# Attention on one core: the first head's two score banks in one maximum instruction, and outputs grouped by query halves

## The chip, the core and the metric

The kernel runs on one core of a Trainium2 chip. A core has TensorE (PE, matrix products from SBUF into PSUM), VectorE (DVE), ScalarE (ACT), GpSimd (POOL) and SyncE (SP, which here only issues DMAs). PSUM has eight banks of 512 f32 per partition. The metric is the device time of one execution in microseconds.

## What is computed

The program is a chain of blocks on 4096 tokens of 256 features: an attention block beside a feed-forward block, then a convolution and recurrence with a gated MLP beside a mixture of experts. The change touches the first attention alone:

```
keys    = einsum('bthk,hik->bthi', xd, tokeys) * scale      # 16 heads of 16 features, 4096 tokens
queries = einsum('bthk,hik->bthi', xd, toqueries) * scale
values  = einsum('bthk,hik->bthi', xd, tovalues)
dot  = einsum('bqhs,bkhs->bhqk', queries, keys)             # 4096 x 4096 for each head
attn = softmax(dot, axis=-1)
out  = einsum('bhqk,bkhs->bqhs', attn, values).reshape(b, t, e)
return out @ W_unify + b_unify
```

## The kernel before

**The tiling.** Phases follow each other: front, select, ffn, attention, unify, router, mlp, experts. Attention works on pairs of heads (`NP` = 8) and chunks of `CH` = 512 queries (`NQ` = 8). One pair and one chunk is a *round*, 64 in all; `r` counts rounds inside a group of two pairs, `g` over all. A round has `U` = 16 *units* `u`; a unit takes 256 keys (two key tiles `j` of 128) for the tile products. Loops are written out, so the order on each engine is the order of the code.

**Two streams of scores.** Softmax subtracts the row's maximum, which must be known before the exponentials. So scores are computed twice. `max_part` (L1122) multiplies 128 queries by 512 keys into one of four banks `SA[0..3]` (`scores_q`): banks 0 and 1 are head 0, banks 2 and 3 head 1. DVE reduces each bank to one maximum a query (`reduce_unit`, L1237), and only then may PE refill it (`sa_free`). This stream runs `LEAD` = 24 units ahead, so that it has no work in the last 24 units. At the end of a round's maxima `negative_max` (L1244) reduces 64 partial maxima to 8, POOL splits them in two parts (`split_max`), and SP carries them through HBM into two extra rows of the query operand.

`score_tile` (L1128) then computes the transposed scores, 128 keys by 512 queries, with the maximum subtracted, into one of three banks `ST[0..2]`; ACT turns each into `probs` (`exps`, L1203), four tiles a unit. A max part on one half of PE's rows and a score tile on the other half are issued as a pair and run side by side.

**The output.** `pv_part` (L1137) multiplies probabilities by values into the one bank `OP`. A product has only 32 output rows (16 features, a row of ones for the denominator, padding), and four of them stand side by side in the 128 rows: head times key tile. An even unit has two such blocks of 256 queries (LOW, HIGH), an odd unit one block of all 512 (ALL). The four groups of 32 rows thus hold, for each head, two partial sums over the even and the odd key tiles. At a round's end ACT copies the bank to `O4` (`copy_parts`, L1199); SP moves the odd part to the even part's partitions (`fetch_other_half`), POOL adds the two (`sum_halves`), and SP stores the sum and the denominators (`store`).

**The order on PE** in a unit is: pair, pair (then LOW, if the unit is even), pair (then ALL, if odd), pair (then HIGH, if even). I call the pairs 0 to 3 by the bank of their max part. The copy stands on ACT in unit 0 of the next round, after its third exponential. PE waits for it in unit 1, before ALL.

**After attention**, unify needs the last round's sums: SP stores them, loads the denominators, DVE takes reciprocals, SP spreads them, and SP's queue then goes on to later chunks' loads.

## Time and profile before

| | us |
|---|---|
| median of three runs | 3851.46 (3850.99 to 3851.89) |
| profiled execution, its own time | 3858.98 |
| its span | 3857.2 |
| PE busy | 3690.4 (96%) |
| DVE busy | 3288.7 (85%) |
| ACT busy | 2631.5 (68%) |
| POOL busy | 449.7 (12%) |
| mean granted clock of PE | 0.98 of full speed |

Busy time is the union of an engine's instructions. They overlap on an engine, since the next starts before the last has drained: a mean length is longer than an engine's busy time divided by the count. In the page's grouped rows stand line, engine, operation, output and input, shapes, count, then busy us and mean ns of one, then the engine's idle us just before these instructions and who ended it. A PE product of f32 operands shows as two records, so four products of `pv_part` are eight.

### The profile page before, as it was taken

How to read it: one execution, taken by the hardware profiler on the slowest of the kernel's cores; microseconds unless marked ns; L12 is line 12 of the kernel's file. 1: busy time of each engine (PE TensorE's matmuls, PEld its weight loads, DVE VectorE, ACT ScalarE, POOL GpSimd, SP SyncE). 2: the span in 40 equal slices, each digit the busy share in tenths (PEclk: the TensorE clock that was granted, in tenths of full speed). 3: DMA queues.
4: the chain of work that ended last, by engine and by line, in shares of the span. 5: the costliest groups of instructions: out<-in, count | busy, mean ns of one | idle time of the engine just before them, and what ended most of it. 6: DMA issues, size and time to landing. Idle time of an engine off the chain costs nothing. (4 is left out here: it accounts for less than half of the span.)

```text
span 3857.2 us, 69935 instructions
## 1 busy us (share of the span) xinstructions
PE 3690.4 (96%) x27262; PEld 1976.3 (51%) x27262; DVE 3288.7 (85%) x5513; ACT 2631.5 (68%) x4940; POOL 449.7 (12%) x395
## 2 busy tenths in 40 slices
PE   8799899999999999999999999999998959999998
PEld 6587333333333333333333333333335648888887
DVE  6567799999999999999999999999975747756664
ACT  3455588888888888888888888888886422213332
POOL 0133200000000000000000000000002224102323
PEclk9899899999999999999999999999999979999999
DMA  4910322022122022113112212211012010014332
GB/s 145 239 29 19 111 25 32 6 33 28 11 25 34 10 23 26 20 13 33 24 10 29 28 10 25 35 9 9 8 33 83 0 53 32 30 37 116 79 80 39
DMA packets 301675, 157.47 MB, mean 41 GB/s; under 512 B 218398, under 2 KB 273508, under 8 KB 298801
## 3 DMA queue, kind: packets, MB, share of 16 engines
q1 hardware_dynamic: 289072, 142.49, 19.7%
q0 software_dynamic: 12288, 10.70, 1.7%
q8 instruction: 207, 3.39, 0.4%
q14 instruction: 108, 0.88, 0.1%
HBM read 86.46 MB, written 64.18 MB: 39 GB/s over the span
## 5 line engine op out<-in xcount | busy, mean ns | idle before, releaser
L1203 ACT ACTIVATE probs<-attention_scores_t_sums 128x512 f32<-128x512 f32 x4096 | 2120.1, 599 | 336.0 <-PE attention_scores_t_sums L1128 335.6
L1237 DVE TENSOR_REDUCE max_parts<-attention_scores_q_sums 128x1 f32<-128x512 f32 x2016 | 1212.5, 681 | 24.2 <-PE attention_scores_q_sums L1122 24.1
L1237 DVE TENSOR_REDUCE attention_max_parts<-attention_scores_q_sums 128x1 f32<-128x512 f32 x1984 | 1191.7, 681 | 9.0 <-PE attention_scores_q_sums L1122 9.0
L1128 PE MATMUL attention_scores_t_sums<-q_operand,k_operand 50*128 50x512 f32 x2048 | 732.4, 447 | 21.6 <-ACTq L1217 13.8
L1128 PE MATMUL attention_scores_t_sums<-attention_q_operand,attention_k_operand 50*128 50x512 f32 x2048 | 724.9, 446 | 6.5 <-ACT probs L1203 6.5
L1122 PE MATMUL attention_scores_q_sums<-attention_k_operand,attention_q_operand 48*128 48x512 f32 x2048 | 726.2, 444 | 3.3
L1122 PE MATMUL attention_scores_q_sums<-k_operand,q_operand 48*128 48x512 f32 x1952 | 695.9, 446 | 3.1
L1137 PE MATMUL attention_o_psum_sums<-probs,v_heads 128*32 128x256 f32 (+1 forms) x6144 | 602.7, 464 | 0.0
L1137 PE MATMUL attention_o_psum_sums<-probs,attention_v_heads 128*32 128x256 f32 (+1 forms) x6152 | 601.4, 463 | 0.0
L1122 PEld LDWEIGHTS attention_scores_q_sums<-attention_k_operand,attention_q_operand 48*128 48x128 f32 x2048 | 324.6, 184 | 525.7 <-DVE max_parts L1237 205.2
L1122 PEld LDWEIGHTS attention_scores_q_sums<-k_operand,q_operand 48*128 48x128 f32 x1952 | 311.3, 185 | 504.3 <-DVE max_parts L1237 200.8
L1128 PEld LDWEIGHTS attention_scores_t_sums<-attention_q_operand,attention_k_operand 50*128 50x128 f32 x2048 | 338.8, 184 | 43.2 <-ACT probs L1203 38.7
L1128 PEld LDWEIGHTS attention_scores_t_sums<-q_operand,k_operand 50*128 50x128 f32 x2048 | 341.7, 185 | 36.0 <-ACT probs L1203 20.4
L1294 POOL TENSOR_TENSOR o_parts<-o_parts,o_other_half 128x512 f32<-128x512 f32 x65 | 83.2, 1280 | 1531.5 <-DMA o_other_half<-o_parts 1531.5
L1137 PEld LDWEIGHTS attention_o_psum_sums<-probs,v_heads 128*32 128x32 f32 x6144 | 121.1, 108 | 216.4 <-issue 168.0
L1137 PEld LDWEIGHTS attention_o_psum_sums<-probs,attention_v_heads 128*32 128x32 f32 x6152 | 121.3, 108 | 215.3 <-issue 167.1
L1862 ACT ACTIVATE mlp_silu<-mlp_gate_sums,mlp_b_gate 128x512 f32<-128x512 f32 x64 | 44.1, 689 | 221.8 <-PE mlp_gate_sums L118 221.8
L118 PE MATMUL experts_out_sums<-experts_w_low,experts_hidden_high 128*128 128x256 f32 x512 | 144.8, 283 | 0.0
L118 PE MATMUL experts_out_sums<-experts_w_high,experts_hidden_high 128*128 128x256 f32 x512 | 143.6, 280 | 0.0
L118 PE MATMUL experts_out_sums<-experts_w_high,experts_hidden_low 128*128 128x256 f32 x512 | 143.6, 280 | 0.0
L2124 ACT ACTIVATE experts_hidden<-experts_hidden_sums,experts_b 128x512 f32<-128x512 f32 x64 | 43.5, 686 | 127.4 <-PE experts_hidden_sums L118 103.5
L2124 ACT ACTIVATE experts_hidden<-experts_hidden_sums,first_expert_b 128x512 f32<-128x512 f32 x64 | 43.5, 687 | 121.4 <-PE experts_hidden_sums L118 121.0
(321 smaller groups left out, 4617.6 us busy)
## 6 DMA issues: line engine op xcount, KB each, us to landing
o_other_half<-o_parts SPq DMA_DIRECT2D x130, 64.0 KB, 2.0
expert_rows<-attention_empty_rows SPq DMA_DIRECT2D x16, 516.0 KB, 5.5
v_scratch<-value_chunk SPq DMA_DIRECT2D x16, 512.0 KB, 4.9
w_whole<-in_L_ffn_ew SPq DMA_DIRECT2D x8, 1024.0 KB, 7.1
experts_w_whole<-in_L_ffn_ew SPq DMA_DIRECT2D x8, 1024.0 KB, 5.6
q_operand<-q_scratch SPq DMA_DIRECT2D x24, 256.0 KB, 4.8
k_operand<-k_scratch SPq DMA_DIRECT2D x24, 256.0 KB, 6.6
attention_q_operand<-q_scratch SPq DMA_DIRECT2D x24, 256.0 KB, 4.8
```

The lines of the kernel that those rows point to most:

```text
L118: mm = nc.tensor.matmul(out, lhs[l], rhs[r], start=first and n == 0, stop=last and n == 2)
L1122: nc.tensor.matmul(SA[2 * h + j][:, :], QOP[b][64 * h:64 * h + ROWS, qt * P:(qt + 1) * P], KOP[b][64 * h:64 * h + ROWS, key:key + CH], sta ...
L1128: nc.tensor.matmul(ST[bank_n][:, :], KOP[b][64 * h:64 * h + ROWS + 2, kt * P:(kt + 1) * P], QOP[b][64 * h:64 * h + ROWS + 2, c * CH:(c + 1 ...
L1137: mm = nc.tensor.matmul(OP[32 * (2 * h + t % 2):32 * (2 * h + t % 2) + 32, queries], VH[b][:, kt, h, :], PR[:, u % 4 * 4 + t, queries], st ...
L1203: nc.scalar.activation(PR[:, tile, :], ST[bank_n][:, :], ACT.Exp).then_inc(st_free, 1)
L1237: nc.vector.tensor_reduce(MPART[par][:, h, u // 4, part:part + 1], SA[b][:, :], AX.X, ALU.max)\
L1294: nc.gpsimd.tensor_tensor(self.O4[par][:, :], self.O4[par][:, :], self.OB[:, :], ALU.add).then_inc(self.summed, 1)
L1862: nc.scalar.activation(G[m % 2], GP[m % 2][:, :], ACT.Silu, bias=BG[:, m:m + 1])\
L2124: nc.scalar.activation(HF[m % 2][:, :], HP[m % 2][:, :], ACT.Relu, bias=B1[k][:, m:m + 1])\
```

## The change

The four `scores_q` banks become one tile of four banks. The maxima of banks 0 and 1 are taken by one instruction of 2 x 512 elements (`reduce_first`), which waits for both banks and frees both. Banks 2 and 3 keep an instruction each (`reduce_rest`). `negative_max` of a round moves behind `reduce_first` of the next round's first unit.

The four row groups of `OP` become head times *query half* (side) in place of head times key tile, and `OP` is 256 columns wide. Both key tiles are summed in PE. An even unit's two blocks are now the key tiles 0 and 1; an odd unit has both, eight products of 256 columns in place of four of 512. With no partial sums left, `fetch_other_half`, `sum_halves` and the tile `OB` go; `store` waits for the copy and issues eight DMAs in place of four. The copy takes 256 columns and stands behind the fourth exponential of unit 0.

```diff
--- before.py
+++ after.py
...
         ST = [ps(f"scores_t{b}") for b in range(NB)]
-        SA = [ps(f"scores_q{b}") for b in range(4)]
-        OP = ps("o_psum")
+        SA = ps("scores_q", [P, 4 * CH])
+        OP = ps("o_psum", [P, CH // 2])
...
-        LOW, HIGH, ALL = slice(0, CH // 2), slice(CH // 2, CH), slice(0, CH)
-        BLOCKS = ({(0, 1): LOW, (1, 1): HIGH}, {(1, 0): ALL})
+        BLOCKS = ({(0, 1): (0,), (1, 1): (1,)}, {(1, 0): (0, 1)})
...
-                    outs.fetch_other_half(sp, g, r % 2)
...
-                    outs.sum_halves(nc, pool, g, r % 2)
...
                 pe.wait_ge(sa_free, 4 * s + 2 * h + j + 1)
-                nc.tensor.matmul(SA[2 * h + j][:, :], QOP[b][64 * h:64 * h + ROWS, qt * P:(qt + 1) * P],
+                nc.tensor.matmul(SA[:, (2 * h + j) * CH:(2 * h + j + 1) * CH], QOP[b][64 * h:64 * h + ROWS, qt * P:(qt + 1) * P],
                                  KOP[b][64 * h:64 * h + ROWS, key:key + CH], start=True, stop=True)\
                     .then_inc(sa_ready, 1)
...
-            def pv_part(b, u, exps, queries):
+            def pv_part(b, u, exps, key_tiles):
 
                 pe.wait_ge(st_free, NB + exps)
-                for t in range(4):
-                    h, kt = 1 - t // 2, 2 * u + t % 2
-                    mm = nc.tensor.matmul(OP[32 * (2 * h + t % 2):32 * (2 * h + t % 2) + 32, queries], VH[b][:, kt, h, :],
-                                          PR[:, u % 4 * 4 + t, queries], start=(u == 0 and queries.start == 0),
-                                          stop=(u == U - 1 and queries.stop == CH))
-                if queries.stop == CH:
+                for j in key_tiles:
+                    for n in range(4):
+                        h, side = 1 - n // 2, n % 2
+                        mm = nc.tensor.matmul(OP[64 * h + 32 * side:64 * h + 32 * side + 32, :], VH[b][:, 2 * u + j, h, :],
+                                              PR[:, u % 4 * 4 + 2 * (1 - h) + j, side * (CH // 2):(side + 1) * (CH // 2)],
+                                              start=(u == 0 and j == 0), stop=(u == U - 1 and j == 1))
+                if j == 1:
                     mm.then_inc(pv_done, 1)
...
-                            if u == 0 and t == 2:
+                            if u == 0 and t == 3:
                                 copy_parts(r % 2, i * NQ + r // 2, 4 + g * U)
...
-            def reduce_unit(par, u, s):
-                for b in range(4):
-                    h, part = b // 2, 2 * (u % 4) + b % 2
-                    dve.wait_ge(sa_ready, 4 * s + b + 1)
-                    nc.vector.tensor_reduce(MPART[par][:, h, u // 4, part:part + 1], SA[b][:, :], AX.X, ALU.max)\
-                        .then_inc(sa_free, 1)
+            def reduce_first(par, u, s):
+                first = 2 * (u % 4)
+                dve.wait_ge(sa_ready, 4 * s + 2)
+                nc.vector.tensor_reduce(MPART[par][:, 0, u // 4, first:first + 2], SA[:, 0:2 * CH].rearrange("p (j k) -> p j k", j=2),
+                                        AX.X, ALU.max).then_inc(sa_free, 2)
+
+            def reduce_rest(par, u, s):
+                first = 2 * (u % 4)
+                for j in range(2):
+                    dve.wait_ge(sa_ready, 4 * s + j + 3)
+                    nc.vector.tensor_reduce(MPART[par][:, 1, u // 4, first + j:first + j + 1], SA[:, (2 + j) * CH:(3 + j) * CH],
+                                            AX.X, ALU.max).then_inc(sa_free, 1)
...
-                        if not (last and s_round >= HALF):
-                            reduce_unit(s_round % 2, s_unit, s)
-                            if s_unit == U - 1:
-                                negative_max(s_round % 2, s, g + (u + LEAD) // U)
+                        has_max = not (last and s_round >= HALF)
+                        if has_max:
+                            reduce_first(s_round % 2, s_unit, s)
+                        if s_unit == 0 and not (last and s_round > HALF):
+                            negative_max((s_round - 1) % 2, s - 1, g + (u + LEAD) // U - 1)
+                        if has_max:
+                            reduce_rest(s_round % 2, s_unit, s)
...
-    def fetch_other_half(self, sp, g, par):
+    def store(self, sp, att_scratch, den_scratch, g, par, pair, c):
         sp.wait_ge(self.copied, g + 1)
         for h in range(2):
-            sp.dma_start(self.OB[64 * h:64 * h + 32, :], self.O4[par][64 * h + 32:64 * h + 64, :]).then_inc(self.rows_in, 16)
-
-    def sum_halves(self, nc, pool, g, par):
-        pool.wait_ge(self.rows_in, 32 * (g + 1))
-        pool.wait_ge(self.copied, g + 1)
-        nc.gpsimd.tensor_tensor(self.O4[par][:, :], self.O4[par][:, :], self.OB[:, :], ALU.add).then_inc(self.summed, 1)
-
-    def store(self, sp, att_scratch, den_scratch, g, par, pair, c):
-        sp.wait_ge(self.summed, g + 1)
-        for h in range(2):
-            sp.dma_start(att_scratch[bass.ds(pair * (2 * D) + h * D, D), c * CH:(c + 1) * CH],
-                         self.O4[par][64 * h:64 * h + D, :]).then_inc(self.stored[par], 16)
-            sp.dma_start(den_scratch[bass.ds(pair * 2 + h, 1), c * CH:(c + 1) * CH],
-                         self.O4[par][64 * h + D:64 * h + D + 1, :]).then_inc(self.stored[par], 16)
+            for side in range(2):
+                row, queries = 64 * h + 32 * side, slice(c * CH + side * (CH // 2), c * CH + (side + 1) * (CH // 2))
+                sp.dma_start(att_scratch[bass.ds(pair * (2 * D) + h * D, D), queries],
+                             self.O4[par][row:row + D, :]).then_inc(self.stored[par], 16)
+                sp.dma_start(den_scratch[bass.ds(pair * 2 + h, 1), queries],
+                             self.O4[par][row + D:row + D + 1, :]).then_inc(self.stored[par], 16)
```

On DVE, `x` rows merge equal neighbours. This is the program around the end of one round's maxima, before:

```order
L1237 TENSOR_REDUCE max_parts<-attention_scores_q_sums 128x1 x32
L1244 TENSOR_REDUCE attention_neg_max<-max_parts 128x8
L1237 TENSOR_REDUCE attention_max_parts<-attention_scores_q_sums 128x1 x64
L1244 TENSOR_REDUCE attention_neg_max<-attention_max_parts 128x8
L1237 TENSOR_REDUCE max_parts<-attention_scores_q_sums 128x1 x20
L1250 RECIPROCAL recip_den<-denominators 128x32
```

And after, two units on either side of the end of the second round:

```order
L1235 TENSOR_REDUCE attention_max_parts<-attention_scores_q_sums 128x2
L1242 TENSOR_REDUCE attention_max_parts<-attention_scores_q_sums 128x1 x2
L1235 TENSOR_REDUCE attention_max_parts<-attention_scores_q_sums 128x2
L1242 TENSOR_REDUCE attention_max_parts<-attention_scores_q_sums 128x1 x2
L1235 TENSOR_REDUCE max_parts<-attention_scores_q_sums 128x2
L1249 TENSOR_REDUCE attention_neg_max<-attention_max_parts 128x8
L1242 TENSOR_REDUCE max_parts<-attention_scores_q_sums 128x1 x2
```

A unit is three maxima (L1235, then two of L1242) in place of four (L1237). The step to `neg_max` (now L1249) stands one instruction further on, between the next round's two-bank maximum and its one-bank ones.

On PE, an odd unit from its pair 2 on (`scores_q2`) and an even unit up to its pair 2, before:

```order
L1122 MATMUL attention_scores_q2_sums<-k_operand0,q_operand0 128x512
L1128 MATMUL attention_scores_t1_sums<-q_operand0,k_operand0 128x512
L1137 MATMUL attention_o_psum_sums<-probs,v_heads0 32x512 x4
L1122 MATMUL attention_scores_q3_sums<-k_operand0,q_operand0 128x512
L1128 MATMUL attention_scores_t2_sums<-q_operand0,k_operand0 128x512
L1122 MATMUL attention_scores_q0_sums<-k_operand0,q_operand0 128x512
L1128 MATMUL attention_scores_t0_sums<-q_operand0,k_operand0 128x512
L1122 MATMUL attention_scores_q1_sums<-k_operand0,q_operand0 128x512
L1128 MATMUL attention_scores_t1_sums<-q_operand0,k_operand0 128x512
L1137 MATMUL attention_o_psum_sums<-probs,v_heads0 32x256 x4
```

The same place after:

```order
L1120 MATMUL attention_scores_q_sums<-k_operand0,q_operand0 128x512
L1126 MATMUL attention_scores_t1_sums<-q_operand0,k_operand0 128x512
L1136 MATMUL attention_o_psum_sums<-probs,v_heads0 32x256 x8
L1120 MATMUL attention_scores_q_sums<-k_operand0,q_operand0 128x512
L1126 MATMUL attention_scores_t2_sums<-q_operand0,k_operand0 128x512
L1120 MATMUL attention_scores_q_sums<-k_operand0,q_operand0 128x512
L1126 MATMUL attention_scores_t0_sums<-q_operand0,k_operand0 128x512
L1120 MATMUL attention_scores_q_sums<-k_operand0,q_operand0 128x512
L1126 MATMUL attention_scores_t1_sums<-q_operand0,k_operand0 128x512
L1136 MATMUL attention_o_psum_sums<-probs,v_heads0 32x256 x4
```

The pairs and the places of the blocks stay; the odd unit's block has eight products of 256 columns in place of four of 512.

On ACT, around the copy in a round's unit 0, before:

```order
L1203 ACTIVATE probs<-attention_scores_t1_sums 128x512
L1203 ACTIVATE probs<-attention_scores_t2_sums 128x512
L1203 ACTIVATE probs<-attention_scores_t0_sums 128x512
L1199 COPY o_parts0<-attention_o_psum_sums 128x512
L1203 ACTIVATE probs<-attention_scores_t1_sums 128x512
L1203 ACTIVATE probs<-attention_scores_t2_sums 128x512
```

And after:

```order
L1202 ACTIVATE probs<-attention_scores_t1_sums 128x512
L1202 ACTIVATE probs<-attention_scores_t2_sums 128x512
L1202 ACTIVATE probs<-attention_scores_t0_sums 128x512
L1202 ACTIVATE probs<-attention_scores_t1_sums 128x512
L1198 COPY o_sides0<-attention_o_psum_sums 128x256
L1202 ACTIVATE probs<-attention_scores_t2_sums 128x512
```

The copy is half as wide and has changed places with the exponential behind it.

## Rows read from the trace of the kernel before

**Rows 1.** Windows, 500 us of attention: length, then busy us (x instructions) by engine.

```profile
1500.00:2000.00 500.00, 495.71 (x4102) 195.46 (x4103) 494.95 (x837) 430.67 (x834) 21.91 (x39) 1.00 0.18 21
```

**Rows 2.** The page's part 5 (its columns are told above): maxima, and loads for the output sums.

```profile
L1237 DVE TENSOR_REDUCE max_parts<-attention_scores_q_sums 128x1 f32<-128x512 f32 x2016 | 1212.5, 681 | 24.2 <-PE attention_scores_q_sums L1122 24.1
L1237 DVE TENSOR_REDUCE attention_max_parts<-attention_scores_q_sums 128x1 f32<-128x512 f32 x1984 | 1191.7, 681 | 9.0 <-PE attention_scores_q_sums L1122 9.0
...
L1137 PEld LDWEIGHTS attention_o_psum_sums<-probs,attention_v_heads 128*32 128x32 f32 x6152 | 121.3, 108 | 215.3 <-issue 167.1
```

**Rows 3.** Tile `attention_neg_max`, POOL's reader: durations in ns, first and last start in us.

```profile
L1097 POOL TENSOR_TENSOR attention_neg_max_split<-attention_neg_max,attention_zero x63: 202/203/206, 452.0 to 2870.5; 128x8 fp32r<-128x8 f32 x63
```

**Rows 4.** Timeline of DVE, 1504 to 1695 us: start, length, instruction, [idle before <-releaser].

```profile
1504.61 23.40 DVE L1237 TENSOR_REDUCE max_parts<-attention_scores_q_sums 128x1 f32<-128x512 f32 x39
1528.31 15.04 DVE L1237 TENSOR_REDUCE max_parts<-attention_scores_q_sums 128x1 f32<-128x512 f32 x25 [0.30 <-PE attention_scores_q_sums L1122]
1543.39 0.22 DVE L1244 TENSOR_REDUCE attention_neg_max<-max_parts 128x8 f32<-128x64 f32 x1
1543.52 23.40 DVE L1237 TENSOR_REDUCE attention_max_parts<-attention_scores_q_sums 128x1 f32<-128x512 f32 x39
...
1582.43 12.04 DVE L1237 TENSOR_REDUCE max_parts<-attention_scores_q_sums 128x1 f32<-128x512 f32 x20
1594.38 0.34 DVE L1250 RECIPROCAL recip_den<-denominators 128x32 f32<-128x32 f32 x1
1594.64 11.38 DVE L1237 TENSOR_REDUCE max_parts<-attention_scores_q_sums 128x1 f32<-128x512 f32 x19
```

**Rows 5.** Timeline of DVE in the phase before attention.

```profile
372.26 1.23 DVE L883 TENSOR_REDUCE ffn_lead_max_parts<-ffn_scores_q_sums 128x2 f32<-128x1024 f32 x1 [1.27 <-PE ffn_scores_q_sums L783]
373.40 0.68 DVE L900 TENSOR_TENSOR ffn_gelu_low<-ffn_gelu,ffn_gelu_high 128x512 fp32r<-128x512 f32 x1
```

**Rows 6.** Timeline of all engines, 1524 to 1529 us: units 0, 1 and 2 of a round.

```profile
1524.13 0.39 PE L1122 MATMUL attention_scores_q_sums<-attention_k_operand,attention_q_operand 48*128 48x512 f32 x1
...
1524.46 0.64 PE L1137 MATMUL attention_o_psum_sums<-probs,attention_v_heads 128*32 128x256 f32 x8
...
1525.03 0.49 PE L1122 MATMUL attention_scores_q_sums<-attention_k_operand,attention_q_operand 48*128 48x512 f32 x1
...
1525.22 0.59 ACT L1199 COPY o_parts<-attention_o_psum_sums 128x512 f32<-128x512 f32 x1 [0.26 <-PE attention_o_psum_sums L1137]
...
1526.36 0.49 PE L1128 MATMUL attention_scores_t_sums<-attention_q_operand,attention_k_operand 50*128 50x512 f32 x1 [0.18 <-ACT probs L1203]
...
1526.78 1.06 PE L1137 MATMUL attention_o_psum_sums<-probs,attention_v_heads 128*32 128x512 f32 x8
...
1527.78 0.50 PE L1122 MATMUL attention_scores_q_sums<-attention_k_operand,attention_q_operand 48*128 48x512 f32 x1
...
1528.12 0.40 PE L1122 MATMUL attention_scores_q_sums<-attention_k_operand,attention_q_operand 48*128 48x512 f32 x1
...
1528.31 1.29 DVE L1237 TENSOR_REDUCE max_parts<-attention_scores_q_sums 128x1 f32<-128x512 f32 x2 [0.30 <-PE attention_scores_q_sums L1122]
...
1528.36 0.39 PE L1122 MATMUL attention_scores_q_sums<-attention_k_operand,attention_q_operand 48*128 48x512 f32 x1
```

**Rows 7.** Timeline of ACT after the last maximum of attention.

```profile
2881.11 1.57 ACT L1203 ACTIVATE probs<-attention_scores_t_sums 128x512 f32<-128x512 f32 x3 [0.17 <-PE attention_scores_t_sums L1128]
...
2885.68 1.58 ACT L1203 ACTIVATE probs<-attention_scores_t_sums 128x512 f32<-128x512 f32 x3 [0.18 <-PE attention_scores_t_sums L1128]
```

**Rows 8.** Timeline of all engines, end of attention and start of unify.

```profile
2921.89 2.36 PE L1137 MATMUL attention_o_psum_sums<-probs,attention_v_heads 128*32 128x256 f32 x24
...
2924.37 0.58 ACT L1199 COPY o_parts<-attention_o_psum_sums 128x512 f32<-128x512 f32 x1 [1.49 <-PE attention_o_psum_sums L1137]
...
2929.17 0.32 SPq L1299 DMA_DIRECT2D attention_scratch<-o_parts  x1
...
2934.10 0.35 DVE L1490 RECIPROCAL unify_last_recip_den<-unify_last_denominators 128x32 f32<-128x32 f32 x1 [0.89 <-DMA unify_last_denominators<-denominator_scratch]
```

More of the change, by code:

```diff
@@ L37 @@
 ROW = C + 2
+STORED = 8 * 16
 class Chain:
@@ L944, in attention_phase @@
         PR, DEN, RD = outs.PR, outs.DEN, outs.RD
-        O4, OB = outs.O4, outs.OB
+        O4 = outs.O4
         MPART = [sb("max_parts0", [P, 2, 4, 8]), lead.MPART]
@@ L1019, in denominators @@
             def denominators(pair, half, even, odd):
-                sp.wait_ge(att_out[0], 64 * (1 + even))
-                sp.wait_ge(att_out[1], 64 * (1 + odd))
+                sp.wait_ge(att_out[0], STORED * (1 + even))
+                sp.wait_ge(att_out[1], STORED * (1 + odd))
                 for h in range(2):
@@ L1069, in _ @@
                 .then_inc(ones_in, 16)
-            sp.wait_ge(vfilled, 5)
+            sp.wait_ge(vfilled, 4)
             rows = DISP.rearrange("(n p r) c -> n p (r c)", p=P, r=4)
@@ L1181, in _ @@
             pe.wait_ge(filled, 1)
-            pe.wait_ge(vfilled, 3)
+            pe.wait_ge(vfilled, 2)
             for n in range(4):
-                nc.tensor.matmul(OP[32 * n:32 * n + 32, :], VH[1][:, 0, 0, :], PR[:, 12 + n, :], start=True, stop=False)
+                nc.tensor.matmul(OP[32 * n:32 * n + 32, :], VH[1][:, 0, 0, :], PR[:, 12 + n, 0:CH // 2], start=True, stop=False)
             def body(i, last):
@@ L1191, in _ @@
             halves(body)
-            pv_part(1, U - 1, count(NP // 2 - 1, HALF - 1, U - 2, 3) + 1, ALL)
+            pv_part(1, U - 1, count(NP // 2 - 1, HALF - 1, U - 2, 3) + 1, (0, 1))
         @block.scalar
@@ L1196, in copy_parts @@
             def copy_parts(par, stored, units):
-                act.wait_ge(att_out[par], 64 * (1 + stored))
+                act.wait_ge(att_out[par], STORED * (1 + stored))
                 act.wait_ge(pv_done, units)
@@ L1218, in _ @@
             for b in range(2):
-                act.sem_inc(att_out[b], 64)
+                act.sem_inc(att_out[b], STORED)
             for t in range(FIRST):
@@ L1275, in __init__ @@
         self.DEN, self.RD = sb("denominators", [P, 32]), sb("recip_den", [P, 32])
-        self.O4 = [sb(f"o_parts{b}", [P, CH]) for b in range(2)]
-        self.OB = sb("o_other_half", [P, CH])
+        self.O4 = [sb(f"o_sides{b}", [P, CH // 2]) for b in range(2)]
         self.AT = [sb(f"attention_t{k}", [P, KC, CH]) for k in range(4)]
```

12 lines of the change are left out of this document (5 added, 7 removed).

## The prediction

> **What bounds the kernel now.** I first asked for the busy time of each engine in a 500 us window of attention: DVE is busy for 494.95 us and PE for 495.71 us [rows 1]. Both look full. PE's figure says little, because the ends of products are modelled and a product that waits for its weights counts as busy. So I went on to what each engine waits for. In the page's grouped rows the 4000 maxima sat idle for 24.2 and 9.0 us in all [rows 2]. A DVE that is almost never without work, for 2400 us, is the bound. The timeline of DVE shows its step: 39 maxima in 23.40 us with a mean length of 0.681 us [rows 2, 4] start (23.40 - 0.68)/38 = 0.598 us apart. Four make a unit of 2.392 us. A round is then 64 x 0.598 = 38.27 us, plus two things in the rows: a wait of 0.30 us, with 0.08 us of draining, at each copy of the outputs, and 0.25 us for `neg_max`. The latter is because it waits for the last maximum to drain: the 25 maxima start at 1528.31, 25 steps are 14.95, and the next round starts at 1543.52 and not at 1543.26. Sum 38.90, and 1543.52 - 1504.61 = 38.91 [rows 4]. The reciprocal, once in four rounds, costs 1594.64 - (1582.43 + 20 x 0.598) = 0.25 us, 0.06 a round. The 63 steps of `neg_max` run from 452.0 to 2870.5, 39.01 us a round over 62 rounds [rows 3], so that 0.05 us a round is spread elsewhere.
>
> **The change, part by part.**
>
> *The two-bank maximum.* Attention before has no such instruction, but the phase ahead of it has the same form: 2 x 512 elements from two banks, 1.23 us long, and the next DVE instruction starts 1.14 us after it [rows 5]. Two single ones take 1.196. So a unit falls from 2.392 to 1.14 + 1.196 = 2.336 us, by 0.056; a round by 0.90. The row reads 0.01 us at best, so the saving lies between 0.045 and 0.065.
>
> The page "VectorE: DVE Perf Modes", section on the TRN2 errata, in the Trainium skill gives a DVE instruction that reads PSUM a fixed cost of 120 cycles at 0.96 GHz, 125 ns; by it a unit would fall by 0.125 us, and the rows, which overlap one instruction's fixed part with the next, show less than half of that.
>
> *`neg_max` behind the next unit's first maximum.* The maxima that it reads have drained by then. What is left is its own step of 0.13 us (1543.39 to 1543.52 [rows 4]) in place of 0.25. If it still drained, nothing would be gained; nothing speaks for more. I take 0.12 a round. POOL and SP get the maximum about 1.3 us later; its rows are wanted 7 units, some 16 us, after that, so it costs nothing.
>
> *PE.* This is the step to doubt, since DVE can only speed up if PE keeps its banks filled. From the start of one thing to the next [rows 6]: pair to pair 0.24 (0.34 when the first follows a block and must load its weights openly), pair to block 0.33 (0.42 if the pair had waited), block of 256 to pair 0.57, block of 512 to pair 1.00. An even unit is 0.24 + 0.33 + 0.57 + 0.34 + 0.33 + 0.57 = 2.38, an odd one 0.34 + 0.24 + 0.33 + 1.00 + 0.34 = 2.25: 4.63 us for two, against DVE's 4.67. PE is just short of the bound. The end of attention, where no maxima are left, gives a check: two units in 2885.68 - 2881.11 = 4.57 us, paced by PE and ACT [rows 7].
>
> The odd unit's block becomes eight products of half the length: the same columns, twice the weight loads. In the last 2.36 us of PE's work three such blocks follow each other: 256 columns twice, then 512 twice, then 512 twice, 24 records [rows 8]. If a group of four side by side streams 512 columns in 0.43 us, that is 0.43 + 0.85 + 0.85 = 2.13 and a tail, with no gap between blocks of one shape. So two halves in a row should cost 1.00 again, at most 2 x 0.57 = 1.14. I take 1.00.
>
> Does the two-bank release fit? Let an odd unit's two-bank maximum start at 0. It ends at 1.23; banks 2 and 3 come free at 1.82 and 2.42; the next two-bank maximum is due at 2.34. PE starts pair 0 at 1.26, pair 1 at 1.60, and a maximum can start about 0.42 after such a pair (0.53 after one with open weights, 1527.78 to 1528.31 [rows 6]): ready at 2.02, 0.32 early. Then block 1.93, pair 2 at 2.50, pair 3 at 2.84, block 3.17, next pair 0 at 3.74 (free since 3.57), pair 1 at 4.08, ready at 4.50 against 4.67. Pair 2 at 4.32 (its bank is free at 4.16), block 4.75, pair 3 at 5.75, ready at 6.28 against 6.41. The following pair 0 is at 6.09, later than its bank's 5.90, so that it no longer waits and its weights load under cover; that gives 0.1 back. The margins are 0.32, 0.17 and 0.13 us: positive and thin.
>
> *The copy.* Now it waits 0.26 us for the block and occupies ACT, and exponential 4, then pair 2's score tile, ALL, and pair 3 are late: this is DVE's 0.30 us [rows 6]. Afterwards exponential 4 goes first, and the copy has half the columns, so between half of 0.59 us and all of it, by a fixed part nearer 0.35. By the schedule above it falls into ACT's gap ahead of the next unit's first tile. I count 0.20 us of DVE waits as left in a round, of the 0.38 before, because the thin margins will cost something; the ends are 0 and 0.38.
>
> *Fetch, sum, store.* The two DMAs and the addition of a round are off the path until the end. There the first store is issued at 2929.17, though the copy ended at 2924.95 [rows 8]. Eight issues in place of four give back part of the 4 us, and DVE's reciprocal waited for this only 0.89 us; that is the most to be won, and I take it. Two copies in the last 24 units, where ACT and PE pace the work, give an estimated 0.5 us each, the 0.26 us of waiting and half a copy. In SP's queue the store stands where it stood, behind the maximum rows, and has 39 us a round.
>
> **The sum.** A round after: 16 x 2.336 + 0.13 = 37.51, with the reciprocal 0.06, the spread 0.05 and the kept waits 0.20 it is 37.82. The gain is 39.01 - 37.82 = 1.19, times 62 rounds 73.8, plus 0.9 and 1.0: 75.7 us. Of the profiled execution's 3859.0 that leaves 3783.3; against the median of the runs, 7.5 us lower, 3775.8. With no waits left it would be 3763, with all 0.38 kept 3787. This is the forecast, 60%.
>
> **Rivals.**
>
> *PE becomes the bound* (27%). For it: the margins of 0.13 and 0.17, and 4.63 against 4.67. If the split block costs 0.14 more, PE needs 4.77 for two units, 38.16 a round, and with the spread 0.05 the gain is 0.80: 50 + 2 us, 3800. Between 3787 and 3806. Against it: PE catches up while DVE does `neg_max` and reciprocals.
>
> *The fixed part is saved whole* (4%). With 0.125 us saved a unit DVE would need 2.267, and PE's 4.63 for two would set 37.0 a round: 2.0 x 62, about 3726. Against it stands the 1.14 us [rows 5]. This is the time that the page's rule above would give.
>
> *Nothing in the end* (4%). Bank 0 waits for bank 1's maximum, so pair 0 starts 0.5 us later than it could; if pair 1 comes 0.25 us later than worked out, at the odd unit's margin of 0.17, DVE waits about what it saves: 3846 to 3859.
>
> *Slower* (5%). The eight extra weight loads of an odd unit take 0.108 us each [rows 2]. If none is covered, two units take 4.63 + 0.86 = 5.49 us on PE, 43.9 a round, and the time is about 4155. It turns into a loss once two units exceed 2 x 39.01/16 = 4.88, at 0.03 us a load. Against it: eight loads of a block lie inside its 0.57 us now.
>
> The page "TensorEngine Tiling (Array Packing)" in the Trainium skill, "Restrictions", says that column tiling turns fast weight loading off; it names no price, and no row here compares the two ways of loading.
>
> **How the numbers follow.** The time is the forecast's. The range reaches from just below 3763 to just above the PE case's 3806 and leaves out the small cases. A measurement here can tell 0.2%, 7.7 us. Faster: 60 + 27 + 4 = 91%; same 4%; slower 5%.
>
> **What would show it.** In the profile after, the DVE timeline should have a two-bank maximum every 2.34 us, `neg_max` every 37.8 us, with 0.13 us from its start to the next maximum, and DVE idle for little more than before ahead of L1235 and L1242. The odd block should run 1.0 us to the next pair; 1.1 or more makes PE the bound, and the idle time ahead of DVE's rows grows to 0.5 us a round or more. The copy should be some 0.35 us, with no DVE wait behind it. The prediction fails if the two-bank maximum's step is not 1.14 us beside PE's writes, or if PE's chain is longer than its parts.

## The result

The changed kernel takes 3754.76 us, median of four runs (3751.24 to 3757.48), against 3851.68 us: a ratio of 0.9747 (95% interval 0.9731 to 0.9764). The prediction was 3775.8 us, 3758 to 3809. The direction and the mechanism were right; the gain is 96.9 us where 75.7 were forecast, and the time lies 3 us below the range.

The two profiled executions differ by more than the medians: 3858.98 us before, 3752.97 after, spans 3857.2 and 3751.2.

The page's grouped rows for the maxima, which answer to [rows 2]; columns as there:

```profile
L1242 DVE TENSOR_REDUCE max_parts<-attention_scores_q_sums 128x1 f32<-128x512 f32 x1008 | 639.5, 671 | 1.5 <-PE attention_scores_q_sums L1120 1.5
L1242 DVE TENSOR_REDUCE attention_max_parts<-attention_scores_q_sums 128x1 f32<-128x512 f32 x992 | 629.3, 671 | 0.0
L1235 DVE TENSOR_REDUCE max_parts<-attention_scores_q_sums 128x2 f32<-128x1024 f32 x504 | 606.1, 1203 | 8.5 <-PE attention_scores_q_sums L1120 8.5
...
L1235 DVE TENSOR_REDUCE attention_max_parts<-attention_scores_q_sums 128x2 f32<-128x1024 f32 x496 | 597.1, 1204 | 0.0
```

The single maxima idled for 1.5 us in all and the two-bank ones for 8.5 us, 10 us in place of 33 us. Only 2.0 us of these lie between 500 and 2700 us, in the steady part. How long a round takes there is read from POOL's reader of `neg_max`, which answers to [rows 3] (durations in ns, first and last start in us):

```profile
L1096 POOL TENSOR_TENSOR attention_neg_max_split<-attention_neg_max,attention_zero x63: 201/202/205, 447.8 to 2768.7; 128x8 fp32r<-128x8 f32 x63
```

62 rounds take 2768.7 - 447.8 us, 37.43 us each, where they took 39.01. That is 1.58 us a round and 97.7 us in all. The timeline of DVE, where `neg_max` of one round falls into the first unit of the next (it answers to [rows 4]; start, length, instruction):

```profile
1419.93 1.21 DVE L1235 TENSOR_REDUCE attention_max_parts<-attention_scores_q_sums 128x2 f32<-128x1024 f32 x1
1421.06 0.20 DVE L1249 TENSOR_REDUCE attention_neg_max<-max_parts 128x8 f32<-128x64 f32 x1
1421.19 1.27 DVE L1242 TENSOR_REDUCE attention_max_parts<-attention_scores_q_sums 128x1 f32<-128x512 f32 x2
1422.38 1.21 DVE L1235 TENSOR_REDUCE attention_max_parts<-attention_scores_q_sums 128x2 f32<-128x1024 f32 x1
1423.51 1.27 DVE L1242 TENSOR_REDUCE attention_max_parts<-attention_scores_q_sums 128x1 f32<-128x512 f32 x2
1424.71 1.21 DVE L1235 TENSOR_REDUCE attention_max_parts<-attention_scores_q_sums 128x2 f32<-128x1024 f32 x1
```

The unit is 1424.71 - 1422.38 = 2.33 us, the two-bank maximum starts the next instruction 1.13 us on, and the next maximum starts 0.13 us after `neg_max`. Between 500 and 2700 us a maximum waits for PE six times, for 2.0 us in all. Counted out, with the mean steps of all units in that stretch, 1.1305 + 0.598 + 0.598 us: 16 units of 2.3265 are 37.22, `neg_max` 0.125 and the reciprocal 0.06 make 37.41 us, against the measured 37.43. DVE has no idle time left that matters.

PE's odd block after, and the next pair (with [rows 6]):

```profile
1454.94 1.07 PE L1136 MATMUL attention_o_psum_sums<-probs,attention_v_heads 128*32 128x256 f32 x16
...
1455.94 0.49 PE L1120 MATMUL attention_scores_q_sums<-attention_k_operand,attention_q_operand 48*128 48x512 f32 x1
```

The split block takes 1.00 us to the next pair, as the long one did. The copy on ACT, in the gap between two units' exponentials:

```profile
1476.77 1.09 ACT L1202 ACTIVATE probs<-attention_scores_t_sums 128x512 f32<-128x512 f32 x2
1477.74 0.38 ACT L1198 COPY o_sides<-attention_o_psum_sums 128x256 f32<-128x256 f32 x1
1478.06 1.57 ACT L1202 ACTIVATE probs<-attention_scores_t_sums 128x512 f32<-128x512 f32 x3
1479.90 2.60 ACT L1202 ACTIVATE probs<-attention_scores_t_sums 128x512 f32<-128x512 f32 x5 [0.26 <-PE attention_scores_t_sums L1126]
```

It takes 0.38 us and waits for nothing. From the last `neg_max` to the first DVE instruction of unify it was 58.92 us before (2870.22 to 2929.14) and is 58.0 now. Before, then after:

```profile
2929.14 1.29 DVE L1458 TENSOR_TENSOR residual<-unify_unified_sums,residual 128x512 f32<-128x512 f32 x2 [58.70 <-PE unify_unified_sums L1394]
...
2768.42 0.22 DVE L1249 TENSOR_REDUCE attention_neg_max<-max_parts 128x8 f32<-128x64 f32 x1
2826.42 1.29 DVE L1455 TENSOR_TENSOR residual<-unify_unified_sums,residual 128x512 f32<-128x512 f32 x2 [57.78 <-PE unify_unified_sums L1391]
```

The profiled pair of executions differs by 106.0 us of span. 97.7 are the rounds and 0.9 is this piece. The first `neg_max` split starts at 447.8 in place of 452.0 [rows 3], 4.2 us; the remaining 3.2 us lie behind attention, in code that the change does not touch, and the profiled execution before was itself 7.3 us above its median.

### The profile page after: what moved, and what is told of

Read it like the earlier page. It is cut to its first block and busy times, and to the rows that moved or that the text cites. A ratio compares the mean times of both kernels' runs of the same rounds, so it can differ in the third digit from the quotient of the medians.

```text
span 3751.2 us, 78142 instructions
## 1 busy us (share of the span) xinstructions
PE 3606.0 (96%) x31366; PEld 2065.3 (55%) x31366; DVE 3212.9 (86%) x4513; ACT 2635.8 (70%) x4940; POOL 366.7 (10%) x329
## 5 line engine op out<-in xcount | busy, mean ns | idle before, releaser
L1126 PE MATMUL attention_scores_t_sums<-q_operand,k_operand 50*128 50x512 f32 x2048 | 702.6, 442 | 15.5 <-ACTq L1216 13.8
L1120 PE MATMUL attention_scores_q_sums<-k_operand,q_operand 48*128 48x512 f32 x1952 | 669.3, 440 | 0.0
L1242 DVE TENSOR_REDUCE max_parts<-attention_scores_q_sums 128x1 f32<-128x512 f32 x1008 | 639.5, 671 | 1.5 <-PE attention_scores_q_sums L1120 1.5
L1242 DVE TENSOR_REDUCE attention_max_parts<-attention_scores_q_sums 128x1 f32<-128x512 f32 x992 | 629.3, 671 | 0.0
L1235 DVE TENSOR_REDUCE max_parts<-attention_scores_q_sums 128x2 f32<-128x1024 f32 x504 | 606.1, 1203 | 8.5 <-PE attention_scores_q_sums L1120 8.5
L1136 PE MATMUL attention_o_psum_sums<-probs,attention_v_heads 128*32 128x256 f32 x8208 | 602.8, 388 | 0.0
L1136 PE MATMUL attention_o_psum_sums<-probs,v_heads 128*32 128x256 f32 x8192 | 602.1, 388 | 0.0
L1235 DVE TENSOR_REDUCE attention_max_parts<-attention_scores_q_sums 128x2 f32<-128x1024 f32 x496 | 597.1, 1204 | 0.0
L1136 PEld LDWEIGHTS attention_o_psum_sums<-probs,v_heads 128*32 128x32 f32 x8192 | 187.6, 108 | 276.6 <-issue 149.3
L1136 PEld LDWEIGHTS attention_o_psum_sums<-probs,attention_v_heads 128*32 128x32 f32 x8208 | 188.1, 108 | 275.2 <-issue 147.1
```

Source lines behind the costliest of these rows:

```text
L1120: nc.tensor.matmul(SA[:, (2 * h + j) * CH:(2 * h + j + 1) * CH], QOP[b][64 * h:64 * h + ROWS, qt * P:(qt + 1) * P], KOP[b][64 * h:64 * h + ...
L1126: nc.tensor.matmul(ST[bank_n][:, :], KOP[b][64 * h:64 * h + ROWS + 2, kt * P:(kt + 1) * P], QOP[b][64 * h:64 * h + ROWS + 2, c * CH:(c + 1 ...
L1136: mm = nc.tensor.matmul(OP[64 * h + 32 * side:64 * h + 32 * side + 32, :], VH[b][:, 2 * u + j, h, :], PR[:, u % 4 * 4 + 2 * (1 - h) + j, s ...
L1235: nc.vector.tensor_reduce(MPART[par][:, 0, u // 4, first:first + 2], SA[:, 0:2 * CH].rearrange("p (j k) -> p j k", j=2), AX.X, ALU.max).th ...
L1242: nc.vector.tensor_reduce(MPART[par][:, 1, u // 4, first + j:first + j + 1], SA[:, (2 + j) * CH:(3 + j) * CH], AX.X, ALU.max).then_inc(sa_ ...
```

## The experiments

Each ran four times beside seven runs of the kernel before on the same chip, whose medians were 3855.41 us (first eight kernels) and 3855.94 us (last four). "Round" is the mean distance of two `neg_max` splits on POOL in the profile. A difference of a few us between two medians says little by itself, since the medians of the kernel before differ by 4 us between the result and these runs; where it matters, the round beside it tells more.

**Only the two-bank maximum** (`pair_only`): `SA` as one tile, `reduce_first` and `reduce_rest`, all else as before:

```diff
...
-                            reduce_unit(s_round % 2, s_unit, s)
+                            reduce_first(s_round % 2, s_unit, s)
+                            reduce_rest(s_round % 2, s_unit, s)
```

> The kernel before with only the two-bank maximum (outputs, fetch, sum, copy and the place of neg_max as before). My theory, that the gain is a sum of a step per unit, neg_max and the copy's wait: the unit falls by 0.065 us, 1000 units, 65 us, and the wait of 0.38 us at each copy stays or grows a little, so 3787 to 3795 us. Rival, that pairing the banks itself removed the wait at the copy: 3760 to 3765 us, with no idle time of DVE behind the copies.

3813.31 us, ratio 0.9895 (0.9876 to 0.9913), round 38.31. Neither theory: the gain is 42 us, two thirds of the 65 that the maxima alone would give. The timeline of DVE behind a copy:

```profile
1430.96 1.20 DVE L1236 TENSOR_REDUCE max_parts<-attention_scores_q_sums 128x2 f32<-128x1024 f32 x1
1432.09 0.67 DVE L1243 TENSOR_REDUCE max_parts<-attention_scores_q_sums 128x1 f32<-128x512 f32 x1
1433.32 0.69 DVE L1243 TENSOR_REDUCE max_parts<-attention_scores_q_sums 128x1 f32<-128x512 f32 x1 [0.56 <-PE attention_scores_q_sums L1122]
1433.92 1.22 DVE L1236 TENSOR_REDUCE max_parts<-attention_scores_q_sums 128x2 f32<-128x1024 f32 x1
```

The unit's last maximum comes 0.63 us later than the step of 0.598 would have it (0.56 is shown as idle, the rest is draining). The unit behind it is 0.06 us too long as well (2.39 us, 1433.92 to 1436.31), and a round without a reciprocal is 1486.28 - 1448.07 = 38.21 us (from `neg_max` to `neg_max`), 0.74 above the 37.47 of its parts. In the kernel before the copy cost 0.38. My reading is that a faster DVE needs the last bank sooner, so that the same delay on ACT and PE costs more of it.

**Only the outputs by query halves** (`sides_only`): the changed kernel with four one-bank maxima a unit and `neg_max` in its old place:

```diff
...
-                            reduce_first(s_round % 2, s_unit, s)
...
-                            reduce_rest(s_round % 2, s_unit, s)
+                            reduce_unit(s_round % 2, s_unit, s)
...
```

> The changed kernel with four one-bank maxima a unit and neg_max in its old place: only the outputs by query halves, with the narrow copy behind the fourth exponential. My theory: the wait at the copy goes (0.38 x 62 = 24 us) with 1 us in unify and up to 4 us at the start, 3822 to 3828 us. Rival, that the wait went because of the banks: 3846 to 3851 us.

3824.70 us, ratio 0.9920 (0.9904 to 0.9937), round 38.59. As my theory had it. DVE goes through 64 maxima without a wait, where it had 39, a wait of 0.30 us, and 25 [rows 4]:

```profile
1453.29 38.34 DVE L1236 TENSOR_REDUCE attention_max_parts<-attention_scores_q_sums 128x1 f32<-128x512 f32 x64
1491.66 0.22 DVE L1243 TENSOR_REDUCE attention_neg_max<-attention_max_parts 128x8 f32<-128x64 f32 x1
```

**The changed kernel with the copy behind the third exponential** (`narrow_copy_early`):

```diff
-                            if u == 0 and t == 3:
+                            if u == 0 and t == 2:
```

> The changed kernel with the copy back behind the third exponential. If the place of the copy removed the wait: 0.2 to 0.4 us of DVE idle time return in each round, 12 to 25 us slower than the changed kernel, 3767 to 3780 us. If its width did: no more than 5 us slower.

3791.14 us, ratio 0.9833 (0.9816 to 0.9849), round 37.96. The place costs 36 us against the changed kernel, more than I expected even if the place decided. The wait is back behind each copy, and the rows show the path on which it comes:

```profile
1419.76 0.37 ACT L1198 COPY o_sides<-attention_o_psum_sums 128x256 f32<-128x256 f32 x1 [0.26 <-PE attention_o_psum_sums L1136]
...
1420.68 0.50 PE L1126 MATMUL attention_scores_t_sums<-attention_q_operand,attention_k_operand 50*128 50x512 f32 x1 [0.16 <-ACT probs L1202]
...
1421.11 1.07 PE L1136 MATMUL attention_o_psum_sums<-probs,attention_v_heads 128*32 128x256 f32 x16
...
1422.11 0.50 PE L1120 MATMUL attention_scores_q_sums<-attention_k_operand,attention_q_operand 48*128 48x512 f32 x1
...
1422.65 0.69 DVE L1242 TENSOR_REDUCE max_parts<-attention_scores_q_sums 128x1 f32<-128x512 f32 x1 [0.35 <-PE attention_scores_q_sums L1120]
```

The copy waits 0.26 us for a block. The exponential behind it (1420.03) ends late, so pair 2's score tile waits for ACT; the block, pair 3 and DVE follow late.

**The changed kernel with `neg_max` behind its own round's last maximum** (`neg_max_at_end`):

```diff
-                        if s_unit == 0 and not (last and s_round > HALF):
-                            negative_max((s_round - 1) % 2, s - 1, g + (u + LEAD) // U - 1)
...
+                            if s_unit == U - 1:
+                                negative_max(s_round % 2, s, g + (u + LEAD) // U)
```

> The changed kernel with neg_max back behind the last maximum of its round. My theory: it drains again and costs 0.25 us in place of 0.125, 62 times, so 8 us slower than the changed kernel, 3762 us. Rival, that draining fell on time that DVE had to wait anyway: no difference.

3761.47 us, ratio 0.9758 (0.9742 to 0.9774), round 37.57: 6.7 us more than the changed kernel, close to the 8 expected; the rounds alone (37.57 and 37.43) make 8 us. The profile shows the draining that came back. The last single maximum starts 0.60 us after the pair's first, at 1460.43, and the next unit at 1461.27, 0.84 later and not 0.60:

```profile
1459.83 1.27 DVE L1242 TENSOR_REDUCE attention_max_parts<-attention_scores_q_sums 128x1 f32<-128x512 f32 x2
1461.13 0.22 DVE L1249 TENSOR_REDUCE attention_neg_max<-attention_max_parts 128x8 f32<-128x64 f32 x1
1461.27 1.22 DVE L1235 TENSOR_REDUCE max_parts<-attention_scores_q_sums 128x2 f32<-128x1024 f32 x1
```

**The kernel before with its wide copy behind the fourth exponential** (`wide_copy_late`). One digit, which is a part of the change that its title does not name:

```diff
-                            if u == 0 and t == 2:
+                            if u == 0 and t == 3:
```

> The kernel before with one thing changed: its copy of 512 columns behind the fourth exponential. If the place decides: the DVE wait behind the copy goes, 24 us faster than before, 3826 to 3832 us. If the place helps only a narrow copy: the wide one still keeps ACT 0.48 us while the next unit's tiles are due, half of the wait stays, 3838 to 3846 us.

3825.62 us, ratio 0.9920 (0.9903 to 0.9937), round 38.60: 29.8 us faster, within 1 us of the whole regrouping of outputs (3824.70). The place decides, also for a copy of 512 columns. Neither the regrouping of the outputs nor the single tile `SA` is needed for it (this kernel has neither), and `narrow_copy_early`, which has both, has the wait. DVE's timeline:

```profile
1490.94 38.35 DVE L1237 TENSOR_REDUCE max_parts<-attention_scores_q_sums 128x1 f32<-128x512 f32 x64
1529.33 0.22 DVE L1244 TENSOR_REDUCE attention_neg_max<-max_parts 128x8 f32<-128x64 f32 x1
```

and the copy on ACT, which no longer waits for the block; a gap like the 0.27 us three exponentials on is there without a copy too (the first row has 0.44):

```profile
1509.22 2.56 ACT L1203 ACTIVATE probs<-attention_scores_t_sums 128x512 f32<-128x512 f32 x5 [0.44 <-PE attention_scores_t_sums L1128]
1511.66 0.59 ACT L1199 COPY o_parts<-attention_o_psum_sums 128x512 f32<-128x512 f32 x1
1512.12 1.61 ACT L1203 ACTIVATE probs<-attention_scores_t_sums 128x512 f32<-128x512 f32 x3
1514.01 2.56 ACT L1203 ACTIVATE probs<-attention_scores_t_sums 128x512 f32<-128x512 f32 x5 [0.27 <-PE attention_scores_t_sums L1128]
```

**The two-bank maximum with the wide copy late** (`pair_wide_copy_late`): both edits together, outputs as before.

> The two-bank maximum alone (as in pair_only) with the copy of 512 columns behind the fourth exponential. Place theory: the 0.74 us a round that the copy cost in pair_only goes nearly whole, 3765 to 3772 us, what remains to the changed kernel being neg_max's 8 us and unify. Width theory: 20 us or more of it stays, above 3785 us.

3764.79 us, ratio 0.9765 (0.9748 to 0.9781). The row of POOL's reader:

```profile
L1097 POOL TENSOR_TENSOR attention_neg_max_split<-attention_neg_max,attention_zero x63: 200/203/206, 447.3 to 2777.0; 128x8 fp32r<-128x8 f32 x63
```

That is 37.58 us a round. Moving the copy is worth 48.5 us here (3813.31 to 3764.79), and 29.8 us without the pairing. The place theory stands. What is left to `neg_max_at_end`, which differs from this kernel by the outputs alone, is 3.3 us. The rounds of the two are alike (37.58 and 37.57), so query halves, the missing fetch and sum and the narrow copy bring nothing in the steady part; that the 3.3 us outside it are theirs is not shown, they are within what two medians differ by.

**Both heads' banks in pairs** (`both_heads_paired`): `reduce_rest` as one instruction over banks 2 and 3:

```diff
-                for j in range(2):
-                    dve.wait_ge(sa_ready, 4 * s + j + 3)
-                    nc.vector.tensor_reduce(MPART[par][:, 1, u // 4, first + j:first + j + 1], SA[:, (2 + j) * CH:(3 + j) * CH],
-                                            AX.X, ALU.max).then_inc(sa_free, 1)
+                dve.wait_ge(sa_ready, 4 * s + 4)
+                nc.vector.tensor_reduce(MPART[par][:, 1, u // 4, first:first + 2], SA[:, 2 * CH:4 * CH].rearrange("p (j k) -> p j k", j=2),
+                                        AX.X, ALU.max).then_inc(sa_free, 2)
```

> The changed kernel with the second head's two banks in one instruction too. DVE then needs 2 x 1.13 = 2.26 us a unit, 36.2 a round with neg_max and reciprocals 36.4. If PE's chain of 4.63 us for two units is right it takes over at 37.0 a round: 3730 us, DVE idle 0.6 us a round. If freeing banks 2 and 3 together makes PE wait in the middle of the odd unit, the time is that of the changed kernel or above, 3755 to 3790 us.

4208.83 us, ratio 1.0915 (1.0896 to 1.0935). Of my two cases the second, but far dearer than I had it. The timeline of DVE and PE over an odd unit (only the rows of the ring):

```profile
1500.12 1.23 DVE L1241 TENSOR_REDUCE max_parts<-attention_scores_q_sums 128x2 f32<-128x1024 f32 x1 [0.95 <-PE attention_scores_q_sums L1120]
...
1501.26 1.22 DVE L1235 TENSOR_REDUCE max_parts<-attention_scores_q_sums 128x2 f32<-128x1024 f32 x1
...
1502.39 1.22 DVE L1241 TENSOR_REDUCE max_parts<-attention_scores_q_sums 128x2 f32<-128x1024 f32 x1
...
1503.52 1.22 DVE L1235 TENSOR_REDUCE max_parts<-attention_scores_q_sums 128x2 f32<-128x1024 f32 x1
...
1503.66 0.50 PE L1120 MATMUL attention_scores_q_sums<-attention_k_operand,attention_q_operand 48*128 48x512 f32 x1 [0.30 <-DVE max_parts L1241]
...
1504.09 1.07 PE L1136 MATMUL attention_o_psum_sums<-probs,attention_v_heads 128*32 128x256 f32 x16
...
1505.09 0.49 PE L1120 MATMUL attention_scores_q_sums<-attention_k_operand,attention_q_operand 48*128 48x512 f32 x1
...
1505.69 1.23 DVE L1241 TENSOR_REDUCE max_parts<-attention_scores_q_sums 128x2 f32<-128x1024 f32 x1 [0.95 <-PE attention_scores_q_sums L1120]
```

Banks 2 and 3 are freed together at 1503.61, when the maximum of 1502.39 ends. Pair 2 starts at 1503.66, then the block of 1.00 us, then pair 3 at 1505.09, and DVE can start 0.60 later, at 1505.69, after 0.95 us idle. From one such start (1500.12) to the next (1505.69) it is 5.57 us for two units, 2.785 a unit: a ring of DVE, pair 2, block, pair 3 and DVE. With single maxima bank 2 is free one maximum (0.6 us) before bank 3, so that pair 2 and the block behind it start sooner, and its next maximum need not wait for pair 3.

**The odd block in 16 products of 128 columns,** in the changed kernel (`odd_blocks_in_quarters`; the loop's body uses `part` and `width`):

```diff
+                        for part in range(2 if len(key_tiles) == 2 else 1):
+                            width = CH // 4 if len(key_tiles) == 2 else CH // 2
...
```

> The changed kernel with the odd unit's block as 16 products of 128 columns in place of 8 of 256: the same columns, twice the weight loads again. If loads are covered by streaming as in the step from 512 to 256: 3755 us. If they are not, PE is slower than DVE's 4.65 us for two units at once: each 0.1 us of the block costs 0.05 us a unit beyond the margin, 3780 us or more.

3754.72 us, ratio 0.9741 (0.9722 to 0.9760), the changed kernel's time. The block and the next pair's start:

```profile
1500.52 1.12 PE L1139 MATMUL attention_o_psum_sums<-probs,attention_v_heads 128*32 128x128 f32 x32
...
1501.57 0.18 PEld L1120 LDWEIGHTS attention_scores_q_sums<-attention_k_operand,attention_q_operand 48*128 48x128 f32 x1 [0.20 <-issue]
```

It takes 1.05 us to the next pair in place of 1.00. The weight loads, twice as many again, are covered all but 0.05 us, and this still fits under DVE. By the prediction's sum PE would now need 4.63 + 0.05 = 4.68 us for two units, more than DVE's 4.65, and yet the steady rounds are the same (most take 37.36 us in both). So that sum was at least 0.03 us too long; its check at the end of attention, 4.57 us, fits better.

**The changed kernel again** (`changed_again`):

> The changed kernel itself, on the chip of the three others: 3755 us, neg_max every 37.43 us.

3754.40 us, ratio 0.9731 (0.9708 to 0.9755), round 37.44 (450.3 to 2771.4).

**One block a unit, between pairs 1 and 2** (`one_block_mid`):

```diff
-        BLOCKS = ({(0, 1): (0,), (1, 1): (1,)}, {(1, 0): (0, 1)})
+        BLOCKS = ({(0, 1): (0, 1)}, {(0, 1): (0, 1)})
...
-                            if u == 0 and t == 3:
+                            if u == 0 and t == 1:
```

> The changed kernel with one block of both key tiles in every unit, between pairs 1 and 2, and the copy behind the second exponential. PE's chain falls from 4.63 us for two units to 0.24 + 0.33 + 1.00 + 0.34 + 0.24 = 2.15 for one. If DVE alone bounds the changed kernel, the time stays, 3752 to 3758 us. If PE bounds it at all, it falls by 5 us or more.

4079.87 us, ratio 1.0584 (1.0553 to 1.0615). I missed by 325 us, and both cases were wrong. The rows (PEld is PE's weight load):

```profile
1500.66 0.50 PE L1126 MATMUL attention_scores_t_sums<-attention_q_operand,attention_k_operand 50*128 50x512 f32 x1
...
1501.22 2.06 ACT L1202 ACTIVATE probs<-attention_scores_t_sums 128x512 f32<-128x512 f32 x4 [0.57 <-PE attention_scores_t_sums L1126]
...
1501.87 0.18 PEld L1126 LDWEIGHTS attention_scores_t_sums<-attention_q_operand,attention_k_operand 50*128 50x128 f32 x1 [0.45 <-ACT probs L1202]
...
1502.29 1.07 PE L1136 MATMUL attention_o_psum_sums<-probs,attention_v_heads 128*32 128x256 f32 x16
...
1503.30 0.50 PE L1126 MATMUL attention_scores_t_sums<-attention_q_operand,attention_k_operand 50*128 50x512 f32 x1
```

Four score tiles now follow each other without a block, and there are three banks for them. The tile of 1500.66 is read by the exponential of 1501.22; only when that ends, 0.60 us later, can the fourth tile of the row, the third after it, load its weights for the same bank (1501.87, after the idle time that ACT ended). Then come the block (1502.29) and the next tile 2 (1503.30): 2.64 us a unit, a ring over ACT. I had summed PE's chain and the ring of the maxima's banks and not looked at the score tiles' ring.

**The same with both heads paired** (`one_block_mid_both_paired`):

> The same with both heads' banks in pairs. By busy time DVE needs 2.26 us a unit and PE 2.15, which would give 36.4 us a round, 3691 us. By the ring of four banks it doesn't: from the start of one two-bank maximum 1.26 us to its release, 0.34 to pair 1, 0.33 + 1.00 over the block, 0.34 to pair 3 and 0.42 until a maximum can start are 3.69 us, and with the other head's 1.13 this makes 4.82 us for two units, 2.41 a unit: 3825 to 3845 us.

4098.32 us, ratio 1.0616 (1.0586 to 1.0646). The tiles' ring sets this too (the profile again shows score tiles waiting for exponentials, 557 times in 1500 us), so it says nothing of the 2.41 us that I had worked out.

**Both heads paired, the odd block behind pair 3** (`both_paired_odd_block_last`): `BLOCKS` with `{(1, 1): (0, 1)}` for odd units.

> The changed kernel with both heads' banks in pairs and the odd unit's block behind pair 3, so that it no longer stands between pairs 2 and 3. Ring theory: the two-unit ring of 5.57 us falls to 1.26 + 0.34 + 0.33 + 1.00 + 0.34 + 0.42 + 1.13 = 4.82 us, 3825 to 3845 us in place of 4209. If instead the two-bank release is slow in itself, it stays above 4100 us.

4007.05 us, ratio 1.0383 (1.0356 to 1.0409), 2.58 us a unit against 2.785. Taking the block out from between pairs 2 and 3 takes 202 of the 454 us away; I had expected 364 to 384. The trace shows that the expected ring binds and that its pieces were priced too low. From one two-bank maximum of head 1 (DVE, 1499.98) it is 1.28 us to pair 2 (1501.26), 0.34 to pair 3, 0.48 to the block (1502.08), 1.00 to pair 0, 0.34 to pair 1 (1503.42), 0.49 to head 0's maximum (1503.91, after 0.34 us idle for PE) and 1.23 to head 1's (1505.14): 5.16 us for two units. The same seven distances, as medians over the odd blocks between 1000 and 2500 us, add up to 5.17 us, 2.58 a unit. My sum had 0.33, 0.42 and 1.13 for the third, sixth and seventh. So freeing two banks at once is not slow in itself, but it closes a ring that is longer than DVE's own 2.26 us a unit, with the block in either place.

None of these beats the changed kernel.

## Why the prediction was right in kind and short in size

**DVE as the bound: right.** It has no idle time left, and PE kept up. PE's margins held: the split block takes 1.00 us, and even 1.05 us changed nothing. Pair 3 behind the odd block starts at 1479.33 in one odd unit of the changed kernel and its maximum at 1479.49 + 0.60 = 1480.09; with the 0.54 us from such a pair to a maximum that waits for it (1422.11 to 1422.65 above) 0.22 us are to spare, where the prediction had 0.13. A block with 32 loads takes only 0.05 us more than one with 16. The Trainium skill's page "TensorE: Matmul & The Clock Gate", section on the array of 16 sub-arrays, says that PE can pull weight loads ahead of products in flight; the rows agree.

**The two-bank maximum: a term 0.15 us a round too small, 9 us in all.** I took a step of 1.14 us from [rows 5], and it is 1.13, the unit 2.3265 us and not 2.336. The row came from an instruction that had stood idle for its operand and lasted 1.23 us; in the stream the same form lasts 1.203 (page rows above). One instruction fewer saves 0.0655 us, a little more than the upper end of 0.065 that I gave.

**`neg_max`: right.** 0.125 us a round forecast as 0.12; taken back alone it costs 6.7 us.

**"I count 0.20 us of DVE waits as left in a round": this is the step that failed, and the largest.** Six short ones, 2.0 us, are left in the 59 rounds between 500 and 2700 us, 0.03 us a round and far too few to come with the copies. They are counted under the spread below, so the 0.20 fall away whole: 12.4 us. My own schedule had put the copy into ACT's gap and given DVE positive margins, and then I charged the margins for being thin. With the waits at 0 the sum in the prediction was 3763, still inside the range; it took the maximum's 9 us too to leave it. The prediction had these 9 us in hand: it gave 0.045 to 0.065 us for the saving and summed with 0.056, but the range's lower end was set just below 3763, as if that term were exact. What the runs add is that the wait at the copy is no fixed 0.38 us: it is a delay on ACT that reaches DVE through the fourth exponential, a score tile, the block and pair 3. At the faster DVE it would have been 0.74 us a round with the wide copy, and 0.52 with the narrow one (37.96 - 37.44). So the move of the copy was worth 48.5 us beside the pairing, more than its price in the profile of before.

**The "spread" of 0.05 us:** 0.02 to 0.03 of it is left, about 1.5 us less.

**Fetch, sum, store and the last copies: 1.9 us forecast,** 0.9 us seen between the last maximum and unify; with all that the regrouping may bring, 3.3 us between `pair_wide_copy_late` and `neg_max_at_end`. Small, as said.

The forecast's 75.7 us and these differences, 9 + 12.4 + 1.5 - 1, make 97.6 us, against 98.6 in the two profiles' rounds and unify and 96.9 between the medians. The 4.2 us at the start vary even with one kernel: the changed kernel again had its first `neg_max` split at 450.3 us in place of 447.8, and its median was the same.

**The rivals.** PE as the bound was ruled out by the quarters. "Slower" by uncovered loads too. "The fixed part is saved whole" is out as well: of the 0.125 us that this rival takes for a merged instruction 0.0655 are saved, a little over half. The "nothing in the end" rival, in which freeing banks together makes DVE wait, is real as a mechanism: it did not bind for head 0, where pairs 0 and 1 follow each other, and pairing head 1 as well costs 454 us, 202 of them because a block stands between its pairs and the rest because the ring is still longer than DVE's step with the block behind pair 3.

## What to carry to other kernels

Where one engine is the bound, price a wait that reaches it by the path that it comes along, and redo that path at the new speed: here the same delay cost the faster engine more (0.74 us and not 0.38), and a move that takes it away was worth more together with the speed-up than alone (48.5 us and 29.8). A sum of an engine's own steps is not its schedule; list each ring of buffers (who fills, who frees, what stands between) and compare the ring's length with the period, before moving a block. And when positive margins have been worked out over the whole ring, do not charge them in the sum as well: give the waits a chance of their own, and let the range take in the uncertainty of every term.

## What the runs showed of the hardware

In the changed kernel a DVE maximum over 512 or 2 x 512 elements of PSUM lasts 0.669 or 1.202 us (medians) when it follows another without a wait, and 0.69 or 1.23 us after idle time. In the kernel before the single one lasts 0.681 us in the stream. The start of the next one behind it is 0.598 and 1.13 us away in every one of these streams, whatever the length reads, so that merging two saves 0.0655 us.

At the start of attention PE ran at half its clock (0.50, 1.2 GHz) for a time that differed. Before, from 430 and from 436 us (columns: length, busy us and count of PE, PEld, DVE, ACT, POOL, then granted clock, DMA share, GB/s):

```profile
430.00:436.00 6.00, 6.00 (x31) 1.93 (x34) 3.27 (x6) 2.97 (x7) 0.00 (x0) 0.50 1.02 403
436.00:442.00 6.00, 6.00 (x32) 2.06 (x28) 3.58 (x7) 3.06 (x7) 0.00 (x0) 0.50 1.03 406
```

After:

```profile
430.00:436.00 6.00, 6.00 (x62) 2.75 (x55) 4.91 (x8) 4.04 (x8) 0.00 (x0) 0.87 1.02 401
436.00:442.00 6.00, 6.00 (x64) 2.75 (x63) 6.00 (x9) 5.25 (x12) 0.00 (x0) 1.00 1.04 390
```

PE had no product at all from 410 to 415 us in either, at a granted clock of 0.50, and was busy throughout from 425 us. Full clock came after 442 us before and at about 431 us after. The first `neg_max` split came at 452.0 and 447.8 us; that the clock alone made this difference is not shown. It started between 447.3 and 450.3 us in six of the kernels with the copy behind the fourth exponential and between 451.7 and 452.7 in the three with the copy behind the third. Outside this order stand 451.8 and 461.6 us, with both heads paired and the copy behind the fourth, and 451.2 and 450.4 us with the copy behind the second; the changed kernel alone gave 447.8 and 450.3. Whether the copy's place has to do with it was not tried.
